# A decoder block with routed experts on one core: gate logits folded into the output product, and the expert stage begun five steps earlier

## What is computed

```
x = layernorm(x + attention(x))                 # 8 heads, mix of three attentions, gated
x = layernorm(x + cross_attention(x, context))  # 16 heads of 8; ends in o @ Wo + bo
x = layernorm(x + moe(x))                       # below

def moe(x):
    t = x * rsqrt(mean(x * x) + eps) * norm_scale
    logits = t @ gate_w + gate_b                # 8 experts
    top_v, top_i = top_k(logits, 2); probs = softmax(top_v)
    sum over the two experts: probs * (swiglu(t @ w1[e] + b1[e]) @ w2[e] + b2[e])
```

## Time and profile before

| | us |
|---|---|
| median of three runs | 633.15 |
| lowest, highest | 630.25, 634.72 |
| the profiled execution | 630.97 |
| its span | 629.0 |
| PE busy | 517.8 (82%) |
| DVE busy | 478.0 (76%) |
| POOL busy | 435.2 (69%) |
| ACT busy | 432.9 (69%) |

### The profile page before, as it was taken

How to read it: one execution, slowest core, us unless ns; L and a number is a source line. 1 busy time by engine, 2 the same in 40 slices (tenths; PEclk the granted TensorE clock), 3 DMA queues, 4 the chain that set the end, 5 groups by cost and what they waited for, 6 DMA issues and landing times.

```text
span 629.0 us, 17434 instructions
## 1 busy us (share of the span) xinstructions
PE 517.8 (82%) x5258; PEld 405.9 (65%) x5258; DVE 478.0 (76%) x1705; ACT 432.9 (69%) x1295; POOL 435.2 (69%) x446
## 2 busy tenths in 40 slices
PE   6678888888888789999999997457677888998862
PEld 3456666666666656777767765447567888887720
DVE  3679999999998776888997896646566468897602
ACT  3789999999998768888977763225334445667703
POOL 6678889898896672665668988673566654687622
PEclk9889999999998999999999998576779889999976
DMA  2256565654542221111111111231122221623152
GB/s 71 63 209 225 213 254 194 240 167 116 160 143 63 57 72 36 44 46 42 40 37 44 40 40 53 53 94 42 50 68 61 67 64 43 208 70 85 50 168 67
DMA packets 71503, 60.69 MB, mean 96 GB/s; under 512 B 21592, under 2 KB 64758, under 8 KB 69110
## 3 DMA queue, kind: packets, MB, share of 16 engines
q1 hardware_dynamic: 66230, 50.03, 26.4%
q0 software_dynamic: 4608, 8.50, 4.1%
q10 hardware_dynamic: 576, 1.05, 0.5%
HBM read 28.50 MB, written 32.08 MB: 96 GB/s over the span
## 4 chain that ended last, share of the span: by engine, by line
PE 43%; DVE 19%; ACT 14%; issue 13%; another core or an unknown queue 5%; POOL 3%; DMA 2%; DVEq 0%; SPq 0%; ACTq 0%; POOLq 0%
ACT l_weights L394 8%; PE ps L1496 5%; PE ps L1476 5%; PE ps L882 4%; PE ps L964 4%; PE ps L871 3%; PE ps L348 3%; PE ps L325 2%; PE ps L337 2%; PE ps L916 2%; PE ps L909 1%; DVE l_shifted L1165 1%; DVE a_ms L527 1%; PE ps L355 1%
## 5 line engine op out<-in xcount | busy, mean ns | idle before, releaser
L1630 POOL DMA_INDIRECT y_dram<-l_keys,l_blk x80 | 80.3, 1003 | 64.5 <-ACT l_keys L1568 41.4
L394 ACT ACTIVATE l_weights<-ps,a_nb,a_rinv 128x64 f32<-128x64 f32 x256 | 99.5, 413 | 3.4 <-DVE a_nb L517 1.7
L817 POOL DMA_INDIRECT disp_dram<-l_R,x_pos x64 | 64.6, 1009 | 17.6 <-issue 17.6
L1074 POOL TENSOR_TENSOR l_keys<-x_kT,l_table 128x1024 f32<-128x1024 f32 x32 | 61.3, 1919 | 4.5 <-PE ps L882 4.5
L483 POOL TENSOR_TENSOR a_rinv<-a_ms,a_halfneg 128x10 f32<-128x10 f32 (+1 forms) x32 | 62.2, 1943 | 2.8 <-DVE a_ms L527 2.0
L1496 PE MATMUL ps<-l_table,l_keys 128*128 x320 | 49.6, 303 | 10.9 <-ACT l_keys L1581 6.3
L394 ACT ACTIVATION_READ_ACCUMULATOR l_weights<-ps,a_nb,a_rinv 128x1 f32 x256 | 54.7, 214 | 0.0
L1496 PEld LDWEIGHTS ps<-l_table,l_keys 128*128 128x128 f32 x320 | 43.1, 209 | 16.4 <-issue 16.1
L1712 DVE TENSOR_SCALAR l_work<-ps 128x512 f32<-128x512 f32 x40 | 27.5, 688 | 34.1 <-PE ps L1476 18.5
L1568 ACT ACTIVATE l_keys<-ps,l_blk 128x128 f32<-128x128 f32 x80 | 25.0, 364 | 40.2 <-PE ps L1496 24.5
L1142 DVE TENSOR_REDUCE x_mx<-ps 128x16 f32<-128x1024 f32 x32 | 39.1, 1222 | 15.0 <-PE ps L882 14.9
(11 more groups left out here) (235 smaller groups left out, 1676.7 us busy)
## 6 DMA issues: line engine op xcount, KB each, us to landing
disp_dram<-l_R SPq DMA_DIRECT2D x16, 1048.0 KB, 4.3
l_blk<-disp_dram SPq DMA_DIRECT2D x80, 65.5 KB
l_shifted<-in_xT SPq DMA_DIRECT2D x32, 64.0 KB, 2.0
l_R<-in_x SPq DMA_DIRECT2D x32, 64.0 KB, 1.9
l_W1h<-v_dram SPq DMA_DIRECT2D x64, 32.0 KB, 2.5
x_dram<-a_xo SPq DMA_DIRECT2D x32, 64.0 KB, 1.8
l_W1l<-in_w SPq DMA_DIRECT2D x4, 512.0 KB
x_xa<-x_dram SPq DMA_DIRECT2D x32, 64.0 KB, 1.8
```

Of the source, the lines that this page charges most:

```text
L394: last = nc.scalar.activation(E[:, e.u4, g, :], ps_Sh[:, g % 2, g // 2, 0:D], ACT.Exp, bias=nb[:, e.u2, g:g + 1], scale=rinv[:, e.u4, g:g ...
L817: nc.gpsimd.indirect_dma_start(out=disp[:, :], out_offset=bass.IndirectOffsetOnAxis(ap=pos[:, B, k_, j:j + 1], axis=0), in_=R[:, t, k_, :] ...
L1074: G.tensor_tensor(KB[:, c.t % 3, :, :, :], kT[:, c.u4, :].rearrange("p (b k) -> p b k", b=2).unsqueeze(2).to_broadcast([P, 2, 8, T]), hm[: ...
L1630: G_.indirect_dma_start(out=Y[:, :], out_offset=bass.IndirectOffsetOnAxis(ap=blk[:, (2 * q + j) % NB, PLACE:PLACE + 1].bitcast(I32), axis= ...
```

## The change

- **The gate is folded into the output product.** The layer norm's row is (r − mean) / deviation, so its product with the gate weights is r times the weights with their mean taken off, over the deviation. r is the input row plus `o @ Wo + bo`. The output product becomes 136 wide (`GATED`): 128 columns of `y` and 8 of gate sums, from `oT @ [Wo | Wo·gw]`, from `x1T @ gw` (hence 12 kept input transposes, not 2) and from a constant in the 8 last columns of `xb`. The turned row, its copy and the logit product go. DVE scales the 8 columns by the inverse deviation and adds the bias (L1227) in the step that writes the row. `Wo·gw` and the constants are made in cross steps 1 to 9.
- **Routing.** Eight batches of four; each of the lags is two steps shorter: phases from lag 12, rank at 15 (PE) and 16 (DVE). The weights are written straight into the row. The table of part 0 moves from step 38 to steps 32 to 35, spread over four.
- **Sends.** One a step in steps 20 to 25, two in 26 to 38, one in 39 to 41; 35 in all, not 39. Row 31 goes in step 38, not 39. The late rows are nine before the first scatter, as before, then three for each two pairs until pair 13.
- **Steps.** `OFFSET` 33, `WEAVE` 39: pair 0 follows cross step 38. From step 39 the turned results and `y` go to the sums' bank (7). New waits come with it: `bank_free`, those in `bank_read`, and from step 41 on PE's output product waits for the experts' weighted result of pair (step − 41).

```diff
-OWN_LAG, CROSS_LAG, OFFSET = 10, 28, 34
-WEAVE = 44
+OWN_LAG, CROSS_LAG, OFFSET = 10, 28, 33
+WEAVE = 39
+GATED = P + 8
...
-    BATCHES = ((0, 8), (8, 8), (16, 4), (20, 4), (24, 4), (28, 4))
+    BATCHES = tuple((t, 4) for t in range(0, tiles, 4))
...
-        placed_rows = 2 * sum(n for t, n in BATCHES if step >= t + n + 18)
-        some = min(placed_rows - sent, 2 if step < tiles + 3 else 3) if step < tiles + 10 else 0
+        placed_rows = 2 * sum(n for t, n in BATCHES if step >= t + n + 16)
+        some = min(placed_rows - sent, 2 if 26 <= step < tiles + 7 else 1) if step < tiles + 10 else 0
...
-    ps_x, ps_y, ps_oT = ps[:, 0, 0:P], ps[:, 0, P:2 * P], ps[:, 0, 2 * P:3 * P]
+    ps_x, ps_oT, ps_y = ps[:, 0, 0:P], ps[:, 0, P:2 * P], ps[:, 0, 2 * P:2 * P + GATED]
+    ps_oT_late, ps_y_late = ps[:, 7, 0:P], ps[:, 7, 512 - GATED:512]
...
+    def bank_free(pe):
+
+        pe.wait_ge(y_added, WEAVE - 10)
+        pe.wait_ge(oT_ready, WEAVE - 9)
+
     def bank_read(pe, n):
 
         if n == 2:
-            pe.wait_ge(lg_kept, tiles)
-            pe.wait_ge(rank_read, len(BATCHES) - 1)
+            pe.wait_ge(rank_read, sum(t + 15 < WEAVE + 2 for t in last_of))
+            pe.wait_ge(oT_ready, tiles)
+            pe.wait_ge(y_added, tiles - 1)
+        if n == 3:
+            pe.wait_ge(y_added, tiles)
+        if n > 2 and WEAVE + n - 16 in last_of:
+            pe.wait_ge(rank_read, last_of[WEAVE + n - 16] + 1)
...
+                if step_of(at) == WEAVE:
+                    pe.wait_ge(normed, tiles)
+                if step_of(at) > WEAVE + 1:
+                    pe.wait_ge(later.y_ready, step_of(at) - WEAVE - 1)
+                ps_y = output_place(at)
...
-                nc.tensor.matmul(ps_y, later.onesb[0:72, :], bo[:, :], start=True, stop=False, skip_group_check=True)
+                nc.tensor.matmul(ps_y[:, 0:P], later.onesb[0:72, :], bo[:, :], start=True, stop=False,
+                                 skip_group_check=True)
+                nc.tensor.matmul(ps_y[:, P:GATED], x1T[:, k.t % 12, :], gw[:, :], start=False, stop=False,
+                                 skip_group_check=True)
                 nc.tensor.matmul(ps_y, oT[:, k.u2, :], wo[:, :], start=False, stop=True,
...
-            if m.live:
-                m.wait(pe, row_ready)
-                m.free(pe, tT_ready, 1)
-                nc.tensor.transpose(ps_t, R[:, m.t, 0, 0:P], idf[:, :]).then_inc(t_turned, 1)
...
+            if step_of(at) == 8:
+                pe.wait_ge(prepared, 2)
+                nc.tensor.matmul(ps_gates[:, 0:8], woT[:, :], gw[:, :], start=True, stop=True)
+                nc.tensor.matmul(ps_gates[:, 8:16], ones[:, :], gw[:, :], start=True, stop=True).then_inc(gate_sums, 1)
...
-            if o.live:
-                if o.t == 0:
-                    pe.wait_ge(prepared, 1)
-                o.wait(pe, tT_ready)
-                nc.tensor.matmul(ps_lg, tT[:, o.u2, :], gw[:, :], start=True, stop=True).then_inc(logits, 1)
...
-            if m.live:
-                m.wait(act, t_turned)
-                m.free(act, logits, 2)
-                nc.scalar.activation(tT[:, m.u2, :], ps_t, ACT.Copy).then_inc(tT_ready, 1)
...
-            d, g, k, l, o, w, v, z, y = (Tile(at, m) for m in (5, 8, 10, 11, 14, 1, 2, 14, 18))
+            d, g, k, l, w, v, z, y = (Tile(at, m) for m in (5, 8, 10, 11, 1, 2, 12, 16))
...
+                lB = batch_of[l.t]
+                V.scalar_tensor_tensor(lg[:, lB % 2, l.t - BATCHES[lB][0], :], r[:, l.u2, P:GATED],
+                                       later.rs[:, l.t, 1:2], later.gb[:, :], ALU.mult, ALU.add).then_inc(lg_kept, 1)
...
+            if w.t == 6:
+                dve.wait_ge(gate_sums, 1)
+                n.add(V.tensor_copy(woT[:, :], ps_woT))
+                n.add(V.tensor_scalar(ones[:, :], ones[:, :], later.bo_col[:, :], None, ALU.mult))
+                n.settle()
+                V.scalar_tensor_tensor(gw[:, :], ps_gates[:, 0:8], -1.0 / P, gates[:, :], ALU.mult,
+                                       ALU.add).then_inc(prepared, 1)
+            if w.t == 8:
+                dve.wait_ge(gate_sums, 2)
+                n.add(V.tensor_copy(xb[:, :, P:GATED], ps_gates[:, 8:16].unsqueeze(1).to_broadcast([P, 8, 8])))
+                n.settle()
+                V.tensor_copy(wo[:, P:GATED], ps_gates[:, 0:8]).then_inc(prepared, 1)
...
+            if TALLY < step_of(at) <= TALLY + 4:
+                table(0, step_of(at) - TALLY)
+            if step_of(at) == tiles + 17:
+                for phase_ in range(1, 5):
+                    table(1, phase_)
...
         def begin():
 
             load_experts(0)
+            later.bank_free(pe)
             turn_rows(0)
-            pe.wait_ge(later.tT_ready, tiles)
             turn_rows(1)
...
-            return 0 if row < 48 else 1 + (row - 48) // 2 if row < 56 else row - 50
+            return 0 if row < 44 else 1 + 2 * (row - 44) // 3
...
-            later.double()
+            later.double(0)
...
+            if p == PA // 2:
+                later.double(1)
```

169 lines of the change are left out of this document (88 added, 81 removed).

## The result

Median of four runs 656.4 us (652.0 to 665.0), the kernel before beside it 631.8 (630.25 to 634.72): ratio 1.036 [1.029, 1.044]. The run of 665.0 us had a mean granted clock of 0.79, the others 0.90 to 0.92, and the ratio is of those others. The forecast was 622.5, with a range of 611 to 634. The profiled executions: 656.77 us (span 655.0) against 630.97 (629.0), 25.8 us apart.

A forecast was written before the change was run, and what follows sets the result against it. PE was taken to bound the cross steps, then PE with DVE, then POOL's pace, with the hand-over weakest. Terms of −2, −1, +2 and −9 us summed to −10: 622.5 us predicted, range 611 to 634.

The forecast's parts named there:

- hand-over: Attention to experts: starting pair 0 after step 38, with the last five steps woven in, gains 9 us (bounds 1 and 14).
- rival A: At the hand-over: it pays little, −1 to −5 us, for a total of 626 to 632; chance 25%.
- 400.5: First expert pair: the time in us at which PE was to turn its fetched rows.
- two old gaps: First expert pairs before the change: unexplained waits of DVE (5.59 us) and ACT (5.42 us); the forecast lay between none and one.
- rival C: Steps 15 to 34: DVE, blocked beside POOL's work, becomes the bound, +14 us, total 635 to 639; chance 10%.
- DVE's routing: Cross steps: eight batches of four put more phases on DVE, +2 us (bounds 0 and +15).
- One step less: Start of the cross attention: OFFSET 33 begins it one step earlier, −2 us (bounds 0 and −4.2).
- PE per tile: Cross steps where PE bounds: less PE work for each tile, −0.11 us a step, −1 us in all (bounds 0 and −3.5).
- The sends: POOL: one send a step in steps 20 to 25 still fits, at 4.9 us of work in 5.4.
- no bound: Expert pairs: POOL's 4.45 us a pair puts result 13 at 475 us or later, against 504.0, so POOL doesn't limit them.
- Rival B: First expert pairs: PE stays at its upper clock level, −7 us more, total 612 to 616; chance 13%.

The follow-up runs named there:

- g1_weave40: f3_table with the expert pairs begun after step 39 instead of step 43: ratio 1.013.
- i2_after4: f3_table with pairs begun after step 38 and late sends moved to two a pair ahead of pairs 4 to 13: 642.0 us, 1.019.
- e3_weave44: The changed kernel with the expert pairs begun after cross step 43 again, nothing else undone: 643.3 us, 1.010.
- e1_spread: The changed kernel with its 29 late rows sent two ahead of each scatter, pairs 0 to 14: 658.8 us, 1.036.
- f3_table: e3_weave44 with 45 rows sent ahead, 19 late, and the whole table of part 0 made in step 38: 633.4 us, 0.995.
- g4_offset34: f4_weave42 with the cross attention begun one step later again (OFFSET 34): ratio 0.991.
- f4_weave42: f3_table with the expert pairs begun after step 41 instead of step 43: 627.2 us, 0.990.
- h2_after4: f4_weave42 with its late rows moved to two a pair ahead of the scatters of pairs 4 to 13: 602.5 us, 1.018.
- e2_ahead: The changed kernel with DVE's batch sums and part 0's table pieces moved ahead of the row's writing: 657.4 us, 1.031.

## Why the prediction was wrong

The step that failed is the **hand-over**, taken as −9 us. It measures −11.5 + 16.3 = +4.8 us to result 4, which lies outside rival A's −1 to −5 as well. What the working put at nothing is the run of nine late sends beside the first pairs.

- *Its first half held.* By the text, result 0 would be at 421 with step 38 at about 390, 31 us apart; it is 30.2 us, 11.5 less than before. Row 31 and the bank weren't in time for "400.5" (the pair turns at 412.01 after a fetch wait of 3.81 us), but step 38 itself was 11.9 us later than before.
- *Its second half failed.* The working had the last power and the first result both "near 421" and "the first scatter at some 435, as before". So by its own numbers nine sends ran beside the first pairs. It gave them no price, since a result may be four pairs ahead of its scatter, and added only 6 us of round trips, 1.3 us of table loads and the question whether two old gaps would come again (5.59 and 5.42 us). The power came at 436.09, 3 us behind result 0, the first scatter at 449.72, and beside them DVE stood for 10.76 us and ACT for 11.87. First to third result took 27.9 us, for 13 to 19 in the forecast and 13.4 before. "Slot 41 waits for the first pair's weighted result on ACT", in the working a part of three round trips of 2 us, is what holds the power back here; g1_weave40 shows that a late power costs without that wait too (result 0 to 4 32.9 us).
- *What the runs put on it.* i2_after4 puts 9 us on the sends; against e3_weave44 the whole early weave costs 11.9 us, all before result 4, and 2.6%.
- *The signs.* Third result 461.07, against the stated limit of 442. From the normalising of tile 31 to the first pair's first DVE operation 5.3 us, for 9 to 10, because that tile's normalising (415.10) itself stood behind the split of the first fetched rows on DVE (414.02). Steps 16 to 20 took 5.8 us each, at the mark for rival C. Result 20 to 39 by first DVE operation 3.77 us a pair, for 3.66. Table loads on ACT five after 400 us, as forecast.

**DVE's routing**, taken as +2 us with bounds 0 and +15: +4.0 in steps 8 to 20 and +10.5 in 30 to 38, so the term was mis-sized, inside its bounds; the second number is high in this execution (e1_spread, with the same steps, has +3.2). The place was wrong too. "In steps 26 to 34 DVE has 42.18 of 50 and POOL sets the pace: 0" trusted a busy share. With PE at 47 of 50 there a single DVE operation that is held for 2.4 us stops PE, and the clock drops. The split of the table, dismissed in one sentence, is some 6 us of it: undone in f3_table, the steps took 30.9 us again, with the batches of four still in. That also tells how far **rival C** was right: the mechanism is real, but the cross steps of the change have five operations of over 1 us that take a fraction of it elsewhere (1.08, 2.49, 2.42, 1.97, 2.78 us), two of them the table's, not one in each step, and it is the smaller half of the loss, 12 of 26.6 us in this execution.

**One step less**, −2: the −2.3 at the first normalised tile agree by luck, since 15 of 17 traces with this `OFFSET` have +0.2 to +2.4 there. What the step alone is worth stays open: whole times could neither show nor refute it (g4_offset34). **PE per tile**, −1: hidden, since DVE was full in that stretch (29.45 of 30 us).

**The sends** and "no bound" for the pairs: the count was of POOL's time alone. Four late rows more cost the kernel before 0.35%, and the stretch from result 4 to 13 follows how many late sends there are for each pair (leaving out the comparison at 593 us): one a pair 42.1 to 47.7 us, three for two pairs 52.3 to 55.3, two a pair 58.2 and 58.7. Apart from these stand the three kernels whose POOL waits over 10 us for a place (50.1 to 55.8, with one a pair). Two pairs took 10.1, 11.9 and 13.5 us from scatter to scatter (kernel before, change, e1_spread), where six, seven and eight indirect DMAs of POOL at 1.27 us are 7.6, 8.9 and 10.2. So each send added its own time and more, where the working took all of POOL's 4.45 us a pair to be hidden.

**Rival B** (the clock stays up) went the other way. From 445 us to the end PE is at its lower level for 61.5 us, before for 40.6, in f4_weave42 for 21.1. This stretch of f4_weave42 is to be read beside the two of the first section:

```profile
450.00:520.00 70.00, 58.90 (x461) 54.53 (x459) 48.33 (x97) 35.06 (x93) 39.86 (x39) 0.95 0.24 65
```

The lower clock comes with the gaps and lengthens the products behind them: a pair's products L1538 take 2.07 us at 475.58 and 1.06 at 481.65. How the +9.9 us from result 4 to the end divide between clock, late rows and the scatters' delay, no run separates.

**Still open.** Why DVE, ACT and PE stand still beside POOL's unbroken runs, and why they don't in h2_after4, where the kernel before took 593 us; and what made the experts of that comparison about a tenth faster (result 19 to 39 65.8 us for 70.8 to 75.6).

## What to carry to other kernels

When a stage's tail is woven into the next, look for the tail's waits on the new stage's results and follow them to the third engine: what that engine does after the tail (here nine sends) is free only while it lies ahead of the new stage's first result. The best starts of the weave were those where the last power still ran 18 to 19 us ahead of it, enough for the twelve sends behind it: two or three steps earlier than before, not five. A small VectorE operation laid beside GpSimd's long multiplication costs that multiplication's rest; where PE is full its place matters more than its size, and moving it up within the step only exposed the next one here. And a stretch of one trace should be looked for in a second trace of the same code before a term is called measured: two rows of the table above did not repeat.

## What the runs showed of the hardware

- *Unbroken runs of indirect sends come with halts.* After: ten sends from 437.01 to 449.41 us, and DVE idle for 10.76 us until 455.34. In f4_weave42 twelve sends run from 415.87 to 430.8, and ACT sits idle for 7.24 us until 433.08; there the halt falls ahead of result 0. In e2_ahead ACT is idle for 17.75 us until 459.20. In i2_after4 only three sends stand behind the last power, and no gap of PE, DVE or ACT is over 5.6 us until result 4. But an unbroken run isn't enough: in h2_after4, where the kernel before took 593 us, 53 indirect DMAs (19 sends, 34 scatters) run from 438.6 to 507.7 us, and no gap of the three is over 5 us. How sends would stop three other engines, no trace shows.
- *A held cast.* The conversion of 128x8 numbers with one input took 1.97 us at 370.96, to the end of POOL's multiplication, and a `tensor_scalar` did likewise (2.60 us at 368.84 in e2_ahead).
